# Loading a routed layer's expert matrices, router and bias row during the attention before it

## The chip, the cores and the metric

The kernel runs on one core of a Trainium2 chip. The metric is the device time of one execution in microseconds (us). Times of the profile are counted from the first instruction of the profiled execution. TensorE is called PE here, VectorE DVE, ScalarE ACT, GpSimd POOL and SyncE SP. SP, ACT and POOL can each issue DMA transfers on a queue of their own (SPq is q1, ACTq is q10).

## The reference

A sequence of 32 batches of 112 tokens with 256 features passes through four layers. Each adds a gated cross attention over a context of 375 rows, and a gated feed-forward part. Only the last layer's two parts and their order matter here:

```python
def _L3_xattn_ref(q, k, v, mask, gamma, beta):          # q: layernorm(x), k = v = context
    logits = jnp.einsum('bsd,btd->bst', q, k) / jnp.sqrt(d_k)
    logits = jnp.where(mask == 0, NEG, logits)
    attn = jax.nn.softmax(logits, axis=-1)
    x = jnp.einsum('bst,btd->bsd', attn, v)
    ...                                                  # layernorm over features
    return xhat * gamma + beta

def _L3_ffn_ref(tokens, router_w, router_b, expert_weights):   # 8 experts of 256 x 256
    logits = jnp.einsum('bsh,eh->bse', tokens, router_w) + router_b
    probs = jax.nn.softmax(logits, axis=-1)
    top_p, top_i = jax.lax.top_k(probs, TOP_K)           # TOP_K = 2
    w = top_p / (jnp.sum(top_p, axis=-1, keepdims=True) + EPS)
    ...
    y_all = jnp.einsum('nh,ehd->ned', x, expert_weights)
    y_k = jnp.take_along_axis(y_all, idx[:, :, None], axis=1)
    out = jnp.einsum('nk,nkh->nh', wf, y_k)
    ...
x = x + jnp.tanh(g_xattn[3]) * _L3_xattn_ref(_layernorm(x), ctx_1024, ctx_1024, mask, ...)
x = x + jnp.tanh(g_ffn[3]) * _L3_ffn_ref(_layernorm(x), router_w, router_b, expert_weights)
```

## The kernel before

x stays in SBUF for the whole program, as `x_sb` with 112 tokens on the partitions and 32 batches of 256 features. Each part of each layer is a function with one or more blocks. In a block every engine has its own hand-written list of instructions, tied to the others by semaphores; at the end of a block all engines wait for each other, and only then does the next block begin. Storage and semaphores of a function are given back at its end (`cleanup_on_exit`). All numbers are float32.

`masked_attention` (line 528) is the fourth attention. PE's list runs over the batches j: transpose the normalised x of batch j + 1 (line 763), transpose the probabilities of batch j - 2 (782), scores of batch j (773), attention product of batch j - 2 (793). DVE masks the scores (651, 655), takes the statistics of the result (663, 665, 667), adds the residual of batch j - 4 (675), normalises batch j + 4 (642) and takes the statistics of batch j + 10 (633, 635). ACT turns the mask into a number (706, 710), does the exponentials (723), and copies the two transposes out of PSUM (717, 731). POOL raises to the power of -1/2 (597 and 599 for groups of four batches, 612, 615, 617 for each result) and adds beta (606).

Its transfers: SP loads for each pair of batches one mask (line 578, 328 KB, three buffers) and for each batch the transposed context `ctx_t` (line 583, 375 KB, four buffers). The load of ctx_t of batch j waits until the scores of batch j - 4 are done. ACT loads the context `ctx_sb` itself (line 736, 384 KB, eight buffers), after the attention product that frees the buffer. That goes on for the last eight batches too, and SP waits at the end of its list (line 590) until all have landed. At its start ACT loads the rows gamma and beta (738, 739), and waits for POOL's `masked` and for the first mask.

`routed_layer` (line 2756) has two blocks. The first, small one prepares: SP issues eight expert matrices into `we` (2776, 256 KB each), ACT loads the router as 8 rows of 256 (2780) and the bias row, repeated on 112 partitions (2781); POOL writes the numbers 0 to 7 (2786), DVE turns them into floats (2791); PE transposes the router (2799), DVE copies it to `rw_t` (2793). The second block is the layer: DVE takes the statistics of 16 batches (2857, 2860), POOL the power (2840, 2842), DVE normalises (2871), PE transposes (2994) and multiplies by the router (3003), ACT copies (2983), DVE finds the two best experts and their weights, then PE multiplies each batch by all eight experts (3015) while DVE adds the weighted results (2935). The other 16 batches are normalised and routed in between.

Of the kernel before, what the change touches and what calls it, by code (L numbers as in the profile page):

```python
# [4 lines left out]
F32 = mybir.dt.float32  # L5
U32 = mybir.dt.uint32
I32 = mybir.dt.int32
# [47 lines left out]
def row(v):  # L55

    return v.rearrange("(a n) -> a n", a=1)
# [470 lines left out]
def masked_attention(k):  # L528
# [8 lines left out]
    with nc.cleanup_on_exit():  # L537
# [34 lines left out]
        with nc.Block() as block:  # L572
            @block.sync
            def _(sp):
# [10 lines left out]
                for j in range(B):  # L585
                    if j % 2 == 0:
                        load_masks(j // 2)
                    load_ctx_t(j)
                for j in range(NB):
                    sp.wait_ge(ctx_loaded[j], 16 * (B // NB))  # L590

            @block.gpsimd
            def _(pool):
# [25 lines left out]
                pool.memset(masked[:, :], MASKED).then_inc(s["masked_ready"], 1)  # L619
                norm_scale(0)  # L620
# [81 lines left out]
            def _(act):  # L702
# [36 lines left out]
                act.dma_start(beta[:, :], row(k.inputs["L3_xattn_beta"]).partition_broadcast(S)).then_inc(s["rows_loaded"], 16)  # L739
                act.wait_ge(s["masked_ready"], 1)  # L740
# [2011 lines left out]
E3 = 8  # L2752
WEIGHT_EPS = 1e-10


def routed_layer(k):
# [3 lines left out]
    with nc.cleanup_on_exit():  # L2760
        we = sb(nc, "we", [P, DC, E3, D], F32)
        rw_t = sb(nc, "rw_t", [P, DC, E3], F32)
        rb = sb(nc, "rb", [S, E3], F32)
        iota = sb(nc, "iota", [S, E3], F32)
        experts_loaded = sem(nc, "experts_loaded")
        with nc.cleanup_on_exit():
            router_loaded = sem(nc, "router_loaded")
            transposed = sem(nc, "transposed")
            iota_ready = sem(nc, "iota_ready")
            rw = sb(nc, "rw", [E3, D], F32)  # L2770
            iota_i = sb(nc, "iota_i", [S, E3], I32)
            with nc.Block() as block:
                @block.sync
                def _(sp):
                    for e in range(E3):
                        sp.dma_start(we[:, :, e, :], k.inputs["L3_ffn_expert_weights"][e]).then_inc(experts_loaded, 16)

                @block.scalar
                def _(act):
                    act.dma_start(rw[:, :], k.inputs["L3_ffn_router_w"]).then_inc(router_loaded, 16)  # L2780
                    act.dma_start(rb[:, :], row(k.inputs["L3_ffn_router_b"]).partition_broadcast(S)).then_inc(router_loaded, 16)
                    act.wait_ge(router_loaded, 32)

                @block.gpsimd
                def _(pool):
                    pool.iota(iota_i[:, :], pattern=[[1, E3]], base=0, channel_multiplier=0).then_inc(iota_ready, 1)

                @block.vector
                def _(dve):
                    dve.wait_ge(iota_ready, 1)  # L2790
                    dve.tensor_copy(iota[:, :], iota_i[:, :])
                    dve.wait_ge(transposed, 1)
                    dve.tensor_copy(rw_t[:, :, :], k.ps[:, 0, 0:DC * E3].rearrange("p (c e) -> p c e", c=DC))

                @block.tensor
                def _(pe):
                    pe.wait_ge(router_loaded, 32)
                    for c in range(DC):
                        mm = pe.transpose(k.ps[:, 0, c * E3:(c + 1) * E3], rw[:, c * P:(c + 1) * P], k.ident[0:E3, 0:E3])
                    mm.then_inc(transposed, 1)  # L2800

# [26 lines left out]
        with nc.Block() as block:  # L2828
# [16 lines left out]
            def _(dve):  # L2845
# [27 lines left out]
                def shift_logits(g):  # L2873
                    cut = slice(g * BODY, (g + 1) * BODY)
                    dve.wait_ge(s["logits_done"], BODY * (g + 1))
# [112 lines left out]
            def _(pe):  # L2988
# [8 lines left out]
                def route(j):  # L2997
                    pe.wait_ge(s["xt_copied"], j + 1)
                    if j >= BODY:
                        pe.wait_ge(s["exps_ready"], j // BODY)  # L3000
# [133 lines left out]
```

## Time and profile before

| | |
|---|---|
| median of 3 runs | 3386.21 us (3382.05 to 3387.3) |
| the profiled execution's own time | 3380.2 us |
| its span, first to last instruction | 3378.5 us |
| busy, share of the span | PE 91%, DVE 60%, ACT 43%, POOL 19% |
| mean granted TensorE clock | 0.947 of full speed |
| the fourth attention's block | 2972.37 to about 3095 us |
| the routed layer's first block | 3096.08 to about 3101.3 us |
| the routed layer's second block | 3102.86 to 3378.5 us |

The profile is one execution; the time of its own stands beside the span so that a difference in the profile can be carried over to the runs. The rows of the next section come from the trace of that execution. A row of the timeline is: start in us, duration in us, engine, line, operation, written tile <- read tiles, shapes, how many instructions were merged, and in brackets the idle time of the engine before it and what ended it. "PEld" is PE's weight load; SPq and ACTq are transfers being issued (the duration is that of issuing, not of moving the data).

### The profile page before, as it was taken

The page shows a single profiled execution, that of the slowest core. Times are in us where ns is not written, and L with a number is a line of the kernel's source. Part 1 is how long each engine was busy: PE and PEld are TensorE (multiplying, and loading weights), DVE is VectorE, ACT ScalarE, POOL GpSimd, SP SyncE. Part 2 cuts the span into 40 slices and gives each one's busy share as a digit, 9 for nine tenths or more (in the row PEclk, how much of TensorE's full clock was granted, in tenths as well). Part 3 has the DMA queues.
Part 4 walks back from the last instruction along what each step waited for, and adds up shares of the span by engine and source line. Part 5 has one row for each costly group of instructions (what it writes and reads, how often), then busy time and mean ns, then how long its engine had stood idle before and what let it go on. Part 6 is the DMA issues. An engine that isn't in the chain of part 4 may idle for free. (4 is left out here: it accounts for less than half of the span.)

```text
span 3378.5 us, 61456 instructions
## 1 busy us (share of the span) xinstructions
PE 3073.2 (91%) x23644; PEld 2339.1 (69%) x23644; DVE 2032.5 (60%) x4425; ACT 1444.9 (43%) x2808; POOL 644.0 (19%) x903
## 2 busy tenths in 40 slices
PE   8986699967789999999999999499999999797999
PEld 6864355634588999999999999366667666465443
DVE  3444211128537788778778777266666666587554
ACT  3421111103325555555555555166666666354000
POOL 3443100028300013012001300411111111144000
PEclk9986799988899999999999999699999999798899
DMA  7661111127710000000000000100000000075000
GB/s 237 190 249 48 51 50 50 50 78 226 256 40 1 2 1 2 1 1 2 2 1 2 2 1 2 39 20 20 20 20 20 20 20 11 4 210 178 12 15 19
DMA packets 75489, 183.40 MB, mean 54 GB/s; under 512 B 12215, under 2 KB 18960, under 8 KB 74866
## 3 DMA queue, kind: packets, MB, share of 16 engines
q1 hardware_dynamic: 56452, 135.91, 12.6%
q10 hardware_dynamic: 12606, 29.06, 2.8%
q0 software_dynamic: 6144, 14.50, 1.5%
q8 instruction: 194, 3.18, 0.4%
q14 instruction: 93, 0.76, 0.1%
HBM read 151.83 MB, written 27.79 MB: 53 GB/s over the span
## 5 line engine op out<-in xcount | busy, mean ns | idle before, releaser
L2313 DVE CUSTOM_DVE_ANT_0 probs<-ps,add 112x375 f32<-112x375 f32 x512 | 250.1, 545 | 58.4 <-PE ps L2441 54.6
L2369 ACT ACTIVATE probs<-probs,neg_top 112x375 f32<-112x375 f32 x512 | 281.7, 599 | 4.6 <-DVE neg_top L2313 3.2
L1864 DVE TENSOR_REDUCE top<-ps 112x16 f32<-112x1792 f32 x96 | 194.4, 2025 | 60.0 <-PE ps L2080 58.4
L3015 PE MATMUL ps<-we,xn_t 128*112 128x512 f32 x512 | 226.9, 605 | 0.5 <-DVE x_sb L2935 0.5
L1217 DVE TENSOR_TENSOR hidden<-gated,ps 128x512 f32<-128x512 f32 x64 | 44.0, 688 | 301.8 <-PE ps L1260 301.8
L2466 PE MATMUL ps<-ident,probs 112*125 112x112 f32 x1536 | 222.5, 281 | 2.8 <-DVE probs_t L2320 2.8
L2320 DVE COPY probs_t<-ps 125x336 f32<-125x336 f32 x256 | 128.9, 504 | 151.4 <-PE ps L2466 151.4
L2466 PEld LDWEIGHTS ps<-ident,probs 112*125 112x125 f32 x1536 | 189.7, 188 | 30.8 <-issue 22.6
L1880 DVE TENSOR_TENSOR probs<-probs,inv_sum 112x1792 f32<-112x1792 f32 x96 | 194.4, 2025 | 3.3
L1868 DVE TENSOR_TENSOR probs<-ps,top 112x1792 f32<-112x1792 f32 x96 | 194.3, 2024 | 3.3
L1876 DVE TENSOR_REDUCE row_sum<-probs 112x16 f32<-112x1792 f32 x96 | 193.9, 2020 | 3.2 <-ACT probs L1966 3.2
L2048 PE MATMUL ps<-ident,probs 112*112 112x112 f32 x1536 | 180.5, 260 | 8.0 <-ACT probs_t L1961 7.3
L2063 PE MATMUL ps<-nodes,wq 128*128 128x224 f32 x768 | 182.9, 361 | 4.4
L3015 PEld LDWEIGHTS ps<-we,xn_t 128*112 128x112 f32 x512 | 92.5, 182 | 131.8 <-issue 115.5
L1961 ACT ACTIVATE probs_t<-ps 112x896 f32<-112x896 f32 x192 | 176.0, 917 | 15.6 <-PE ps L2048 4.3
L2039 PE MATMUL ps<-wv,nodes 128*112 128x256 f32 x768 | 181.4, 379 | 0.0
L2048 PEld LDWEIGHTS ps<-ident,probs 112*112 112x112 f32 x1536 | 162.9, 134 | 25.8 <-issue 8.0
L2065 PE MATMUL ps<-att_t,wo 128*128 128x224 f32 x768 | 177.4, 354 | 0.0
L2019 PE MATMUL ps<-nodes,wkh 128*128 128x224 f32 x768 | 172.5, 368 | 0.0
L2935 DVE SCALAR_TENSOR_TENSOR x_sb<-ps,weight,x_sb 112x256 f32<-112x256 f32 x256 | 110.6, 478 | 99.0 <-PE ps L3015 98.7
L1857 DVE COPY v<-ps 112x512 f32<-112x512 f32 x96 | 66.4, 692 | 171.3 <-PE ps L2039 171.3
L2375 ACT ACTIVATE probs_t<-ps 125x336 f32<-125x336 f32 x256 | 115.2, 450 | 125.8 <-PE ps L2466 124.2
(402 smaller groups left out, 6388.0 us busy)
## 6 DMA issues: line engine op xcount, KB each, us to landing
ctx_t<-in_ctx_T_dram SPq DMA_DIRECT2D x128, 375.0 KB, 3.4
ctx_sb<-in_ctx_dram ACTq DMA_DIRECT2D x72, 384.0 KB, 4.9
ctx_sb<-in_ctx_dram SPq DMA_DIRECT2D x32, 384.0 KB
queue<-zeros SPq DMA_DIRECT2D x32, 256.0 KB, 4.2
rows<-queue SPq DMA_DIRECT2D x16, 512.0 KB, 4.2
outputs<-out SPq DMA_DIRECT2D x16, 512.0 KB, 2.6
mask_in<-in_mask_BxSxS_fk_dram SPq DMA_DIRECT2D x16, 328.1 KB, 4.3
mask_in<-in_mask_BxSxS_ik_dram SPq DMA_DIRECT2D x16, 328.1 KB
```

The costliest lines, as they stand in the source:

```text
L1864: dve.tensor_reduce(top[:, :, :], scores, AX.X, ALU.max).then_inc(s["top_done"], 1)
L1868: dve.tensor_tensor(probs[:, m % 2, :, :, :], scores, top[:, :, :].unsqueeze(3).broadcast_to([S, 4, PAIR * HQ, S]), ALU.subtract).then_inc ...
L1876: dve.tensor_reduce(row_sum[:, :, :], p, AX.X, ALU.add).then_inc(s["sum_done"], 1)
L1880: dve.tensor_tensor(p, p, inv_sum[:, :, :].unsqueeze(3).broadcast_to([S, 4, PAIR * HQ, S]), ALU.mult).then_inc(s["probs_normed"], 1)
L2039: mm = pe.matmul(k.ps[0:S, ODD, b * D:(b + 1) * D], node_v[:, i, b * S:(b + 1) * S], w.wv[:, c, i, :], start=i == 0, stop=i == DC - 1)
L2048: mm = pe.transpose(k.ps[0:S, PT + h // 4, h % 4 * S:(h % 4 + 1) * S], probs[:, m % 2, h % 4, b * HQ + h // 4, :], k.ident[0:S, 0:S])
L2063: pe.matmul(k.ps[:, ODD, a * PS:(a + 1) * PS], w.wq[:, c, i, cut], node_q[:, i, :], start=i == 0, stop=False)
L2065: mm = pe.matmul(k.ps[:, ODD, a * PS:(a + 1) * PS], w.wo[:, c, i, cut], att_t[:, i, :], start=False, stop=i == DC - 1)
L2313: dve.tensor_tensor_reduce(out=probs[:, u, h, :], in0=k.ps[0:S, SCORE + h, 0:L], in1=add[:, j % 2, :], scale=1.0, scalar=BIG, op0=ALU.add, ...
L2369: act.activation(probs[:, u, h, :], probs[:, u, h, :], ACT.Exp, bias=neg_top[:, u, h:h + 1], scale=-1.0).then_inc(s["probs_done"], 1)
L2466: mm = pe.transpose(k.ps[0:KR, PT + h % 2, r * S:(r + 1) * S], probs[:, n % 3, h, r * KR:(r + 1) * KR], k.ident[0:S, 0:S])
L3015: mm = pe.matmul(k.ps[0:S, Y + at % YB, :], xn_t[:, j + u, c, :], we[:, c, e:e + TWO, :].rearrange("p e d -> p (e d)"), start=c == 0, stop ...
```

## The change

The storage of the expert matrices, the router, the bias row and the numbering is allocated before the fourth attention instead of after it. SP issues one expert matrix after each ctx_t of batches 17, 19, ... 31. ACT issues router and bias row at the start of the attention, behind gamma and beta. POOL writes the numbering there and turns it into floats itself. The router is laid out transposed by the host, as 128 partitions of 2 x 8 numbers, so that PE's two transposes and DVE's copy fall away. The routed layer's first block is gone; its second block waits for the loads where it first uses them.

```diff
--- before.py
+++ after.py
@@ -525,7 +525,26 @@
                         attend(j - 2)
 
 
-def masked_attention(k):
+E3 = 8
+WEIGHT_EPS = 1e-10
+
+
+def routed_storage(k, r):
+
+
+    nc = k.nc
+    r.we = sb(nc, "we", [P, DC, E3, D], F32)
+    r.rw_t = sb(nc, "rw_t", [P, DC, E3], F32)
+    r.rb = sb(nc, "rb", [S, E3], F32)
+    r.iota = sb(nc, "iota", [S, E3], F32)
+    r.iota_i = sb(nc, "iota_i", [S, E3], I32)
+    r.experts_loaded = sem(nc, "experts_loaded")
+    r.router_loaded = sem(nc, "router_loaded")
+    r.iota_ready = sem(nc, "iota_ready")
+    r.iota_copied = sem(nc, "iota_copied")
+
+
+def masked_attention(k, r):
 
 
     nc = k.nc
@@ -586,6 +605,9 @@
                     if j % 2 == 0:
                         load_masks(j // 2)
                     load_ctx_t(j)
+                    if j >= B - 2 * E3 and j % 2:
+                        e = (j - B + 2 * E3) // 2
+                        sp.dma_start(r.we[:, :, e, :], k.inputs["L3_ffn_expert_weights"][e]).then_inc(r.experts_loaded, 16)
                 for j in range(NB):
                     sp.wait_ge(ctx_loaded[j], 16 * (B // NB))
 
@@ -617,6 +639,9 @@
                     pool.tensor_tensor(gain[:, cut], sum_sq[:, cut], k.neg_half[0:S, 0:1], ALU.pow).then_inc(s["gain_done"], 1)
 
                 pool.memset(masked[:, :], MASKED).then_inc(s["masked_ready"], 1)
+                pool.iota(r.iota_i[:, :], pattern=[[1, E3]], base=0, channel_multiplier=0).then_inc(r.iota_ready, 1)
+                pool.wait_ge(r.iota_ready, 1)
+                pool.tensor_copy(r.iota[:, :], r.iota_i[:, :]).then_inc(r.iota_copied, 1)
                 norm_scale(0)
                 norm_scale(1)
                 for j in range(B + LAG):
@@ -737,6 +762,8 @@
 
                 act.dma_start(gamma[:, :], row(k.inputs["L3_xattn_gamma"]).partition_broadcast(S)).then_inc(s["rows_loaded"], 16)
                 act.dma_start(beta[:, :], row(k.inputs["L3_xattn_beta"]).partition_broadcast(S)).then_inc(s["rows_loaded"], 16)
+                act.dma_start(r.rw_t[:, :, :], k.inputs["L3_ffn_router_w"]).then_inc(r.router_loaded, 16)
+                act.dma_start(r.rb[:, :], row(k.inputs["L3_ffn_router_b"]).partition_broadcast(S)).then_inc(r.router_loaded, 16)
                 act.wait_ge(s["masked_ready"], 1)
                 add_mask(0)
                 copy_xn(0)
@@ -2749,56 +2776,11 @@
                 pipeline(PAIRS, [(transpose, 0), (add_bias, 1), (multiply, 1)])
 
 
-E3 = 8
-WEIGHT_EPS = 1e-10
-
-
-def routed_layer(k):
+def routed_layer(k, r):
 
 
     nc = k.nc
     with nc.cleanup_on_exit():
-        we = sb(nc, "we", [P, DC, E3, D], F32)
-        rw_t = sb(nc, "rw_t", [P, DC, E3], F32)
-        rb = sb(nc, "rb", [S, E3], F32)
-        iota = sb(nc, "iota", [S, E3], F32)
-        experts_loaded = sem(nc, "experts_loaded")
-        with nc.cleanup_on_exit():
-            router_loaded = sem(nc, "router_loaded")
-            transposed = sem(nc, "transposed")
-            iota_ready = sem(nc, "iota_ready")
-            rw = sb(nc, "rw", [E3, D], F32)
-            iota_i = sb(nc, "iota_i", [S, E3], I32)
-            with nc.Block() as block:
-                @block.sync
-                def _(sp):
-                    for e in range(E3):
-                        sp.dma_start(we[:, :, e, :], k.inputs["L3_ffn_expert_weights"][e]).then_inc(experts_loaded, 16)
-
-                @block.scalar
-                def _(act):
-                    act.dma_start(rw[:, :], k.inputs["L3_ffn_router_w"]).then_inc(router_loaded, 16)
-                    act.dma_start(rb[:, :], row(k.inputs["L3_ffn_router_b"]).partition_broadcast(S)).then_inc(router_loaded, 16)
-                    act.wait_ge(router_loaded, 32)
-
-                @block.gpsimd
-                def _(pool):
-                    pool.iota(iota_i[:, :], pattern=[[1, E3]], base=0, channel_multiplier=0).then_inc(iota_ready, 1)
-
-                @block.vector
-                def _(dve):
-                    dve.wait_ge(iota_ready, 1)
-                    dve.tensor_copy(iota[:, :], iota_i[:, :])
-                    dve.wait_ge(transposed, 1)
-                    dve.tensor_copy(rw_t[:, :, :], k.ps[:, 0, 0:DC * E3].rearrange("p (c e) -> p c e", c=DC))
-
-                @block.tensor
-                def _(pe):
-                    pe.wait_ge(router_loaded, 32)
-                    for c in range(DC):
-                        mm = pe.transpose(k.ps[:, 0, c * E3:(c + 1) * E3], rw[:, c * P:(c + 1) * P], k.ident[0:E3, 0:E3])
-                    mm.then_inc(transposed, 1)
-
         stats = sb(nc, "stats", [S, B, 6], F32)
         mean_var = sb(nc, "mean_var", [S, B, 2], F32)
         var_eps = sb(nc, "var_eps", [S, B], F32)
@@ -2873,8 +2855,10 @@
                 def shift_logits(g):
                     cut = slice(g * BODY, (g + 1) * BODY)
                     dve.wait_ge(s["logits_done"], BODY * (g + 1))
+                    if g == 0:
+                        dve.wait_ge(r.router_loaded, 32)
                     link(dve.tensor_tensor(logits[:, cut, :], k.ps[0:S, LOGITS, 0:BODY * E3].rearrange("p (g e) -> p g e", g=BODY),
-                                           rb[:, :].unsqueeze(1).broadcast_to([S, BODY, E3]), ALU.add))
+                                           r.rb[:, :].unsqueeze(1).broadcast_to([S, BODY, E3]), ALU.add))
                     link(dve.tensor_reduce(top[:, cut], logits[:, cut, :], AX.X, ALU.max))
                     link(dve.tensor_tensor(logits[:, cut, :], logits[:, cut, :], each(top[:, cut]), ALU.subtract))
                     dve.sem_inc(s["exps_ready"], 1)
@@ -2899,7 +2883,9 @@
 
                 def pick(g):
                     cut = slice(g * BODY, (g + 1) * BODY)
-                    every = iota[:, :].unsqueeze(1).broadcast_to([S, BODY, E3])
+                    if g == 0:
+                        dve.wait_ge(r.iota_copied, 1)
+                    every = r.iota[:, :].unsqueeze(1).broadcast_to([S, BODY, E3])
                     dve.tensor_tensor(route1[:, cut, :], every, each(best_f[:, cut, 0]), ALU.is_equal)
                     link(dve.tensor_tensor(weight[:, cut, :], every, each(best_f[:, cut, 1]), ALU.is_equal))
                     link(dve.tensor_tensor(weight[:, cut, :], weight[:, cut, :], route1[:, cut, :], ALU.add))
@@ -2996,11 +2982,13 @@
 
                 def route(j):
                     pe.wait_ge(s["xt_copied"], j + 1)
+                    if j == 0:
+                        pe.wait_ge(r.router_loaded, 32)
                     if j >= BODY:
                         pe.wait_ge(s["exps_ready"], j // BODY)
                     at = j % BODY * E3
                     for c in range(DC):
-                        mm = pe.matmul(k.ps[0:S, LOGITS, at:at + E3], xn_t[:, j, c, :], rw_t[:, c, :], start=c == 0, stop=c == DC - 1)
+                        mm = pe.matmul(k.ps[0:S, LOGITS, at:at + E3], xn_t[:, j, c, :], r.rw_t[:, c, :], start=c == 0, stop=c == DC - 1)
                     mm.then_inc(s["logits_done"], 1)
 
                 def experts(j):
@@ -3012,7 +3000,7 @@
                                 pair, w = divmod(before, E3)
                                 pe.wait_ge(s["added"], pair * E3 * 2 + (w // 2 * TWO + TWO - 1) * 2 + w % 2 + 1)
                             for c in range(DC):
-                                mm = pe.matmul(k.ps[0:S, Y + at % YB, :], xn_t[:, j + u, c, :], we[:, c, e:e + TWO, :].rearrange("p e d -> p (e d)"),
+                                mm = pe.matmul(k.ps[0:S, Y + at % YB, :], xn_t[:, j + u, c, :], r.we[:, c, e:e + TWO, :].rearrange("p e d -> p (e d)"),
                                                start=c == 0, stop=c == DC - 1)
                             mm.then_inc(s["experts_done"], 1)
 
@@ -3021,7 +3009,7 @@
                         transpose(j)
                     if j:
                         route(j - 1)
-                pe.wait_ge(experts_loaded, 16 * E3)
+                pe.wait_ge(r.experts_loaded, 16 * E3)
                 for j in range(0, BODY, 2):
                     experts(j)
                     if 4 <= j < 8:
@@ -3068,8 +3056,10 @@
         searched_network(k)
         many_headed_attention(k)
         ternary_layer(k)
-        masked_attention(k)
-        routed_layer(k)
+        r = Fields()
+        routed_storage(k, r)
+        masked_attention(k, r)
+        routed_layer(k, r)
         finish(k)
 
 
@@ -3094,6 +3084,8 @@
 
     if name in _BY_CHUNK:
         a = a.reshape(a.shape[:-2] + (-1, P, a.shape[-1])).swapaxes(-3, -2)
+    elif name == "L3_ffn_router_w":
+        a = a.T.reshape(-1, P, a.shape[0]).swapaxes(0, 1)
     elif name in _COLUMNS:
         a = a.reshape(a.shape[:-1] + (-1, P)).swapaxes(-2, -1)
     elif name in _MASKS:
```

`Fields` is an empty class that holds attributes. In the host's arrangement `_arranged`, arrays in `_BY_CHUNK` (the expert matrices among them) already have 128 rows on the partitions.

## Rows read from the trace of the kernel before

**Rows 1.** The page's chain by engine; then the chain in order of time, from 3040 us

```profile
PE 7%; DVE 1%; POOL 0%; issue 0%; ACT 0%; DVEq 0%
...
3102.81 0.04 issue
3102.86 0.75 DVE stats L2857 x2
```

**Rows 2.** Timeline, end of the attention and the routed layer's first block

```profile
3089.91 2.43 ACTq L736 DMA_DIRECT2D ctx_sb<-in_ctx_dram  x2
3090.46 1.52 PE L793 MATMUL ps<-ctx_sb,probs_t 125*112 125x256 f32 x6 [0.59 <-issue]
3094.01 0.48 DVE L675 SCALAR_TENSOR_TENSOR x_sb<-o_scaled,gain,x_sb 112x256 f32<-112x256 f32 x1 [0.44 <-POOL gain L617]
3096.08 5.24 SPq L2776 DMA_DIRECT2D we<-_ffn_expert_weights_dram  x8
3096.09 0.14 POOL L2786 IOTA iota_i<- 112x8 int32 x1 [2.11 <-POOLq L537]
3096.41 0.34 ACTq L2781 DMA_DIRECT2D rb<-in_L_ffn_router_b_dram  x1
3100.26 0.38 PE L2799 MATMUL ps<-ident,rw 8*128 8x8 f32 x2 [8.29 <-DMA rb<-in_L_ffn_router_b_dram]
3100.68 0.17 DVE L2793 COPY rw_t<-ps 128x16 f32<-128x16 f32 x1 [4.24 <-PE ps L2799]
```

**Rows 3.** SP's waits at line 590: duration ns min/median/max, first and last start us

```profile
L590 SPq EVENT_SEMAPHORE  x4: 17/28/28, 3089.6 to 3094.9; - x4
```

**Rows 4.** Timeline, start of the attention's block

```profile
2972.77 0.45 ACTq L739 DMA_DIRECT2D beta<-in_L_xattn_beta_dram  x1
...
2974.72 0.24 POOL L597 TENSOR_SCALAR var_eps<-mean_var 112x4 f32<-112x4 f32 x1 [2.25 <-DVE mean_var L635]
...
2976.90 0.52 ACT L706 ACTIVATE size<-mask_in 112x375 f32<-112x375 int32 x1 [11.31 <-DMA mask_in<-in_mask_BxSxS_ik_dram]
...
2979.03 2.81 PE L773 MATMUL ps<-ctx_t,xn_t 128*112 128x375 f32 x4 [1.44 <-DMA ctx_t<-in_ctx_T_dram]
```

**Rows 5.** ACT's queue, 3096 to 3110 us, then 2971 to 2980: packets, MB, share

```profile
q10 hardware_dynamic: 144, 0.01, 0.9%
...
q10 hardware_dynamic: 256, 0.23, 13.1%
```

**Rows 6.** Windows: us, busy us (x) of PE PEld DVE ACT POOL, PEclk, DMA share, GB/s

```profile
3020.00:3070.00 50.00, 49.55 (x218) 34.32 (x217) 47.13 (x140) 34.43 (x90) 33.28 (x66) 1.00 0.92 277
3060.00:3070.00 10.00, 10.00 (x48) 7.46 (x47) 8.72 (x25) 7.29 (x19) 7.12 (x15) 1.00 0.97 297
3070.00:3080.00 10.00, 10.00 (x48) 7.46 (x47) 8.34 (x25) 6.88 (x18) 5.80 (x13) 1.00 0.72 227
3101.00:3104.00 3.00, 0.00 (x0) 0.00 (x0) 1.15 (x6) 0.00 (x0) 0.00 (x0) 0.50 1.09 363
```

**Rows 7.** Timeline: mask and ctx_t issues of the steady state, and their users

```profile
3021.12 4.00 SPq L583 DMA_DIRECT2D ctx_t<-in_ctx_T_dram  x2
3066.57 0.43 SPq L578 DMA_DIRECT2D mask_in<-in_mask_BxSxS_ik_dram  x1
3069.47 3.59 SPq L583 DMA_DIRECT2D ctx_t<-in_ctx_T_dram  x2
3078.37 0.51 ACT L706 ACTIVATE size<-mask_in 112x375 f32<-112x375 int32 x1
3081.09 1.43 PE L773 MATMUL ps<-ctx_t,xn_t 128*112 128x375 f32 x4
```

**Rows 8.** DMA issues, 3020 to 3092 us: count, KB, median us to landing

```profile
ctx_sb<-in_ctx_dram ACTq DMA_DIRECT2D x23, 384.0 KB, 3.8
```

**Rows 9.** Windows as in rows 6: the clock at the seam and in the routed layer

```profile
3094.00:3095.00 1.00, 0.00 (x0) 0.00 (x0) 0.48 (x1) 0.00 (x0) 0.00 (x0) 0.65 0.28 108
3179.00:3180.00 1.00, 1.00 (x11) 1.00 (x11) 0.64 (x2) 0.65 (x2) 0.00 (x0) 0.82 0.00 0
3179.64:3186.46 6.82, 6.82 (x26) 4.79 (x26) 0.83 (x2) 1.43 (x4) 0.00 (x0) 0.50 0.00 0
```

## The prediction

> **What bounds the kernel now.** I read the page first. Its chain that ended last holds only about 8% of the span [rows 1], and the time order of that chain says why: its first piece is at 3102.81 us, right ahead of the first statistics instruction of the routed layer. What lies before is separated from it by the end of a block, where every engine waits for every other and no single releaser is recorded. So the program is a row of blocks, and the change touches two of them and the seam between them. All before 2970 us stays as it is, and so does the body of the routed layer: it starts with vector statistics at 3102.86 [rows 1] and runs until 3378.5. Time can change in three places: the start of the fourth attention, its steady state, and the seam.
>
> Then the timeline of the seam [rows 2]. PE's last product of the attention ends at 3091.98; its last vector work, the residual of batch 31, runs 3094.01 to 3094.49. SP leaves its last wait, for the last context transfer, at 3094.9 [rows 3], so this transfer and not an engine ends the block, and 1.2 us later (3096.08) SP, ACT and POOL begin the small inner block. There ACT issues the router and the bias row, PE has to wait 8.3 us until the bias row has landed, transposes at 3100.26, VectorE copies at 3100.68. SP meanwhile spends 5.24 us on issuing eight expert transfers, until 3101.32. After that 1.49 us pass to 3102.81. Two chains are therefore almost equally long: load, transpose, copy (until 3100.85) and SP's issuing (until 3101.32). The change removes both; taking away only one would have bought next to nothing.
>
> Last the attention block, for what the moved work meets there: the start [rows 4], and the busy windows of the steady state [rows 6]. Between 3020 and 3070 PE is busy 49.55 of 50 us and VectorE 47.13, so they set the pace, but the DMA engines are busy 0.92 of the time, 0.97 in the last ten of these. That is where moved transfers could hurt.
>
> **The change part by part.**
>
> *The seam.* The inner block goes wholly: two PE transposes, two copies on VectorE, one iota, ten DMA issues and one block end. If the routed layer's block starts where the inner block started, the gain is 3102.81 - 3096.08 = 6.73 us. What could differ is the price of the seam: 1.2 us from SP's release to the first instruction at this one, 1.49 us from SP's last issue at the next. With the larger one the gain is 6.4. I take 6.7, since the block that ends before the routed layer is now the attention's own, whose 1.2 us stand in the trace. The last context transfer still gates it: it is on ACT's queue, issued by 3092.34 (3089.91 + 2.43, [rows 2]), when all experts have long been loaded.
>
> *ACT's two moved issues* go behind gamma and beta, whose issues end at 2973.22 (2972.77 + 0.45, [rows 4]). Two issues of about 0.34 us [rows 2] end at 2973.9. Behind them on ACT is the first mask operation, at 2976.90 and waiting for its transfer: 3.0 us of cover, cost nothing. Uncovered they would cost 0.7.
>
> *Their packets.* The router is now 128 pieces of 64 bytes, the row 112 of 32 bytes: 240 packets, 15 on each of 16 engines. They compete with the first ctx_t, for which PE stands idle at 2979.03 [rows 4], so this is on the path. Price of a packet: in the inner block ACT's queue had 144 such small ones for 0.9% of 16 engines over 14 us, 14 ns each; at the attention's start 256 of mostly 1 KB took 13.1% of 9 us, 74 ns each [rows 5]. That gives 0.2 to 1.1 us. I take 0.2, because the first row is the row of this very bias transfer.
>
> *POOL's iota and copy* (0.14 us [rows 2] and, as the nearest row, 0.24 for a 112x4 operation [rows 4]) with a wait between them end by about 2973.1. Behind them is the epsilon addition of the first norm scale, at 2974.72 and waiting for VectorE. Cover 1.6 us, cost nothing; uncovered 0.4, and even then xn would only be later at a PE which waits until 2979.03 anyway.
>
> *SP's eight expert issues*, 0.655 us each (5.24 / 8, [rows 2]), come behind ctx_t of batches 17, 19, ... 31, from about 3025 (the pair of rows that starts with batch 16 is issued from 3021.12 for 4.00 us, [rows 7]) to 3073. Each stands ahead of a mask load and of SP's wait for the next scores. The last mask is issued at 3066.57 and used by ACT at 3078.37, the ctx_t of batch 30 issued at 3069.47 and used by PE at 3081.09 [rows 7]: 11.8 and 11.6 us, of which a transfer of this size takes 3.8 to land [rows 8]. Some 7.8 us are spare; 0.66 is nothing.
>
> *Their bytes* are the doubtful term. Seven of them, 1.84 MB, fall in 3025 to 3070: 41 GB/s on top of 277, so 318 GB/s. At 277 GB/s for a share of 0.92 [rows 6] full use is 301 GB/s; 17 GB/s too few over 45 us leaves 0.76 MB, and transfers would be 2.5 us late by 3070. At 3070 to 3080 the load falls to 0.72 and the backlog drains. 2.5 is less than 7.8, so PE sees nothing: cost 0. The other end is that the full engine time of 2.10 MB, 7.0 us at 301 GB/s, comes through to PE. I take the low end, as experts by themselves ran at 363 GB/s [rows 6], so 301 is a cautious limit. The Trainium skill ("Trainium Kernel Development and Optimization", Key Constraints) speaks against this part: transfers issued from SP, ACT and POOL all run on the same 16 engines and interleave, so another queue gives no bandwidth. The share of 0.92 with two queues bears it out. "DMA: Bandwidth & Descriptors" (Specifications) puts the memory's limit for one core at about 358 GB/s; by that figure there would be no backlog at all and the sum the same, by the row's 301 there is one of 2.5 us, hidden.
>
> *New waits* (one on PE, two on VectorE) find semaphores that are set long before; SP's like instructions show 17 to 28 ns [rows 3]. Under 0.1 us in all, nothing taken.
>
> **Sum.** -6.7 + 0.2 = -6.5 us. The profiled execution took 3380.2 us, which makes 3373.7. The median of the runs, 3386.21, is 6.0 above that execution and becomes 3379.7, or 0.19% less. Three runs of one kernel lie 0.16% apart (3382.05 to 3387.3), so about 0.2%, 6.8 us, is what a measurement of this kernel can tell from no change. The forecast sits just under that line.
>
> **Rivals.**
>
> *Contention leaks.* Between 2 and 7 us of the expert transfers' engine time reach PE, as waits of the scores for ctx_t. For it: the shares of 0.92 and 0.97. Against it: 7.8 us of spare lead, and transfers that land in 3.8 us under the present load [rows 8]. With the middle, 4.5 us, the time is 3384.2.
>
> *Clock steps.* In the routed layer the granted clock falls from 1.00 to 0.50 (from 2.4 to 1.2 GHz) twice for 6.8 us, the first time from 3179.64 to 3186.46 [rows 9], after a stretch of small transposes and routing products. PE is saturated there, so each costs half its length, 3.4 us. If the earlier start makes one more, the time is 3383.1; if it saves one, 3376.3. For it: what stands before a fall is a thin stretch of PE work, and such a stretch needs to be only slightly thinner or denser. Against it: the body of the layer is the same instruction by instruction, and after the seam PE is cold in both (its idle stretch goes from 21 to about 14.5 us, and before it fell inside 3094 to 3095 [rows 9], within 3 us of its last product). The Trainium skill ("TensorE: Matmul & The Clock Gate", the part on the clock gate) says that the activity watch is free-running, so that one kernel's slow matmuls vary from run to run; no row of a single execution can show that.
>
> *The end on the other side.* ctx_t comes late often enough that PE stops at each expert, and the clock falls too. It decides when a ctx_t needs more than the 11.6 us of lead, three times what it takes now. Then all 7.0 us come through and, with two falls of 3.4, 13.8: 3386.2 - 6.5 + 13.8 = 3393.5.
>
> *The seam is not shortened*: the 1.49 us and the wait for code or for the barrier are owed to the start of the routed layer itself and come on top of the attention's own seam. Then 1.5 us of the 6.7 stay, and the time is 3381.2. For it: the unexplained difference of 0.3 between the two seams. Against it: the seam at 3096.08 is one full block end and costs 1.2.
>
> **How the numbers follow.** Forecast 0.60 (own range 3377 to 3383, from the 1.1 us bound of the packets, the 0.3 of the seam and half the spread of the runs); contention leaks 0.12; one clock step more 0.08, one less 0.08; seam not shortened 0.07; slower side 0.05. Leaving out the last, and of the others the outer ends (a full leak of 7.0 us, a saved step on top of a fast median), gives 3375 to 3386; that leaves about 0.15 outside. Faster by over 0.2%, that is under 3379.4: a little under half of the forecast (0.27), all of the saved clock step (0.08) and 0.05 from the other cases by the scatter of the medians: 0.40. Slower by over 0.2%, over 3393.0: 0.03, most of the case on the other side. Within: 0.57.
>
> **What would show it.** Right: no matmul or copy between the attention's last residual and the first statistics, and that gap 1.6 us instead of 8.4; expert transfers from about 3025 on; PE without waits for ctx_t; DMA share near 1 from 3025 to 3070; the attention's residual of batch 31 ending within 0.5 us of 3094.5. Wrong: PE waits on ctx_t or ACT on mask_in after 3025, a seam of over 2 us, ctx_t first used later than 2979.5, or a third cold stretch in the routed layer.

## The result, and the profile after

The changed kernel takes 3379.1 us (median of 17 runs, 3374.8 to 3381.64) against 3383.64 for the kernel before (17 runs beside it, 3381.18 to 3387.3): ratio 0.9982, 95% interval 0.9975 to 0.9989, or 6.1 us less, between 3.7 and 8.5. The two medians alone differ by 4.5 us. Its profiled execution has a span of 3373.0 us, 5.5 less than before.

The timeline at the seam, changed kernel, answering to [rows 2]:

```profile
3090.78 2.43 ACTq L761 DMA_DIRECT2D ctx_sb<-in_ctx_dram  x2
...
3094.88 0.48 DVE L700 SCALAR_TENSOR_TENSOR x_sb<-o_scaled,gain,x_sb 112x256 f32<-112x256 f32 x1 [0.44 <-POOL gain L639]
3097.39 0.75 DVE L2839 BATCH_NORM_STATS2 stats<-x_sb 112x6 f32<-112x256 f32 x2 [2.03 <-PEq L556]
```

SP's last wait there, answering to [rows 3]:

```profile
L612 SPq EVENT_SEMAPHORE  x4: 17/28/28, 3090.6 to 3096.2; - x4
```

The start of the attention, where ACT issues four rows, POOL numbers and copies, and PE takes up the first scores, answering to [rows 4]:

```profile
2973.54 0.43 DVE L658 BATCH_NORM_STATS2 stats<-x_sb 112x6 f32<-112x256 f32 x1 [0.87 <-PEq L2605]
2973.55 0.14 POOL L642 IOTA iota_i<- 112x8 int32 x1
2973.76 0.19 POOL L644 CAST iota<-iota_i 112x8 f32<-112x8 int32 x1
...
2974.86 0.45 ACTq L766 DMA_DIRECT2D rb<-in_L_ffn_router_b_dram  x1
...
2975.86 0.24 POOL L619 TENSOR_SCALAR var_eps<-mean_var 112x4 f32<-112x4 f32 x1 [1.91 <-DVE mean_var L660]
...
2979.90 2.81 PE L800 MATMUL ps<-ctx_t,xn_t 128*112 128x375 f32 x4 [1.16 <-ACT xn_t L742]
```

Two windows of the steady attention, answering to [rows 6], and one of SP's new issues:

```profile
3020.00:3070.00 50.00, 49.46 (x219) 34.44 (x218) 47.44 (x141) 33.85 (x89) 33.24 (x66) 1.00 0.98 303
3060.00:3070.00 10.00, 10.00 (x47) 7.41 (x46) 9.04 (x26) 7.47 (x20) 6.93 (x15) 1.00 1.00 320
```

```profile
3026.03 0.66 SPq L610 DMA_DIRECT2D we<-_ffn_expert_weights_dram  x1
```

Four pieces make up the 5.5 us of the spans. I measure each from an instruction that both kernels have. Up to the attention's first statistics nothing is changed, and the changed kernel is 1.13 us late (2973.54 against 2972.41). The attention, first statistics to last residual, takes 121.82 against 122.08, 0.26 less. The seam takes 2.03 (3095.36 to 3097.39) against 8.37 (3094.49 to 3102.86), 6.34 less. The routed layer from its first statistics on takes 275.61 against 275.64. So 1.13 - 0.26 - 6.34 - 0.03 = -5.5. The 1.13 is scatter: in nine executions of the groups in which the kernel before takes some 3385 us, of kernels that are the same up to there, the attention's first statistics began between 2972.4 and 2979.7 us. That is more than the change is worth, and the reason why the experiments below are read by stages and not by spans.

### The profile page after: what moved, and what is told of

Read it like the earlier page. It is cut to its first block and busy times, and to the rows that moved or that the text cites. A ratio compares the mean times of both kernels' runs of the same rounds, so it can differ in the third digit from the quotient of the medians.

```text
span 3373.0 us, 61429 instructions
## 1 busy us (share of the span) xinstructions
PE 3067.9 (91%) x23642; PEld 2335.7 (69%) x23642; DVE 2032.2 (60%) x4423; ACT 1445.8 (43%) x2808; POOL 645.3 (19%) x904
```

## The experiments

Kernels were run in groups, each beside runs of the kernel before on the same chip. The kernel before takes some 3385 us in some of the groups and 3357 to 3360 in others, so that spans are compared only within a group; stages agree across them. This table gives for each execution: attention from first statistics to last residual; seam from there to the routed layer's first statistics; SP's last wait after the end of the last context issue; and the routed layer from its first statistics.

| | attention | seam | last wait | routed layer |
|---|---|---|---|---|
| before | 122.08 | 8.37 | 2.6 | 275.6 |
| before again | 121.97 | 8.48 | 2.7 | 275.7 |
| the change | 121.82 | 2.03 | 3.0 | 275.6 |
| the change again | 121.85 | 2.13 | 3.1 | 275.5 |
| experts moved alone | 121.83 | 6.71 | 3.2 | 277.3 |
| router moved alone | 121.98 | 8.84 | 3.1 | 275.6 |
| experts in the routed block | 121.98 | 2.26 | 3.2 | 275.5 |
| extra block end | 122.08 | 3.32 | 3.0 | 277.2 |
| no unused context | 121.86 | 1.02 | - | 275.9 |
| experts twice | 128.62 | 2.17 | 3.2 | 275.6 |
| experts four times | 139.05 | 2.24 | 3.2 | 275.5 |
| experts twice, spread | 121.66 | 2.18 | 3.2 | 275.6 |
| small loads eight times | 126.42 | 1.70 | 2.7 | 278.4 |

The last kernel below, statistics early, has no statistics at the head of its routed layer and is described by itself. Where the routed layer took over 277 us, a stretch at half clock lasted longer (*the clock steps*, below).

**Experts moved alone.** The router's path stays in a block of its own, as in the kernel before.

```diff
-                pool.iota(r.iota_i[:, :], ...)
-                act.dma_start(r.rw_t[:, :, :], ...)
-                act.dma_start(r.rb[:, :], ...)
+            with nc.Block() as block:     # before the routed layer's block
+                    act.dma_start(rw[:, :], k.inputs["L3_ffn_router_w"]).then_inc(router_loaded, 16)
+                    act.dma_start(r.rb[:, :], ...).then_inc(router_loaded, 16)
...
```

> The expert matrices are loaded during the attention as in the change, but router, bias row and numbering keep the small block of their own, with PE's transposes and VectorE's copies. Theory (the gain is the seam, where two chains ran side by side, SP's issuing of 5.24 us and the bias row's load, transpose and copy of about 4.8 us): taking away SP's alone leaves the other, so from the attention's last residual to the first statistics there are still about 6.5 to 8 us instead of 8.4, and the kernel is 0.5 to 1.8 us faster than before. Rival (the expert loads were the costly part, since the bias row's transfer of 3.5 KB only took so long because it shared the queues with them): the gap falls to under 6 us and at least half of the 6.3 us is had.

Ratio to before 1.0002 (0.9992 to 1.0011). The timeline of this kernel's small block:

```profile
3098.23 0.33 ACTq L2788 DMA_DIRECT2D rb<-in_L_ffn_router_b_dram  x1
3100.61 0.38 PE L2806 MATMUL ps<-ident,rw 8*128 8x8 f32 x2 [7.49 <-DMA rb<-in_L_ffn_router_b_dram]
3101.03 0.17 DVE L2800 COPY rw_t<-ps 128x16 f32<-128x16 f32 x1 [2.77 <-PE ps L2806]
3102.35 0.75 DVE L2864 BATCH_NORM_STATS2 stats<-x_sb 112x6 f32<-112x256 f32 x2 [1.15 <-PEq L2779]
```

The seam keeps 6.71 of 8.37 us. The bias row was used 2.4 us after its issue here against 3.9 with the experts in flight [rows 2], so the rival is right that the transfers hindered each other, but only by 1.5 us; the seam stays over 6. Experts alone earn a quarter of the seam's gain. The expected 0.5 to 1.8 us of the whole time did not show: by the interval, anything from 2.7 us less to 3.7 more is possible, and the profiled execution had one of the longer stretches at half clock.

**Router moved alone.** The small block holds only SP's eight issues.

```diff
-                    if j >= B - 2 * E3 and j % 2:      # in the attention
...
+                    for e in range(E3):                # in a block of its own
+                        sp.dma_start(r.we[:, :, e, :], ...).then_inc(r.experts_loaded, 16)
```

> The other half alone: router, bias row and numbering come from the attention as in the change, and a small block between the two layers holds nothing but SP's issuing of the eight expert transfers. Theory (either chain alone holds the seam): the small block lasts 5.24 us for the issuing and 1.5 us for its end, so from the last residual to the first statistics there are about 8.4 us again, as in the kernel before, give or take 0.5 for the landing of the last context transfer; the run is within 0.1% of before. Rival (the router's path was the longer chain): the gap is under 7.5 us.

Ratio 0.9995 (0.9986 to 1.0005), seam 8.84. The timeline shows SP's issues and what follows the block's end:

```profile
3103.78 5.23 SPq L2787 DMA_DIRECT2D we<-_ffn_expert_weights_dram  x8
```

```profile
3110.47 0.75 DVE L2844 BATCH_NORM_STATS2 stats<-x_sb 112x6 f32<-112x256 f32 x2 [8.84 <-PEq L2781]
```

From the end of SP's issuing, 3109.01, to these statistics at 3110.47 it is 1.46 us, against 1.54 in the kernel before (3101.32 to 3102.86). SP's issuing alone holds the whole seam: each chain was enough for most of it, and only moving both gives it up.

**Experts in the routed block.** The change, but with the eight issues at the head of SP's list in the routed layer's block.

```diff
-                    if j >= B - 2 * E3 and j % 2:      # in the attention
...
             def _(sp):                                 # routed layer
+                for e in range(E3):
+                    sp.dma_start(r.we[:, :, e, :], ...).then_inc(r.experts_loaded, 16)
                 for j in range(0, B, 2):
```

> Router, bias row and numbering are prepared in the attention, no small block, but SP issues the eight expert transfers at the start of the routed layer's own block, ahead of its waits for stores. Theory: nothing waits for the end of the issuing or for the transfers (PE needs them some 27 us later, they take about 10), so the gap stays at about 2.0 us and the time is that of the change within 0.3 us in the trace; DMA share of the steady attention back at 0.92. If the transfers in the attention had cost something hidden there, this one would be faster in the attention's block by that.

Ratio 0.9978 (0.9968 to 0.9988), seam 2.26, DMA share back at 0.91 in the attention, whose length does not move. The span was expected within 0.3 us of the change's and is 2.2 longer, of which 1.9 lie ahead of the attention, where the kernels are the same. So what counted was that no block ends behind the issues, not that the attention carries them.

**Extra block end.** The change with a further block that does nothing.

```diff
+            with nc.Block() as block:
+                    sp.sem_inc(seam, 1)
+                    sp.wait_ge(seam, 1)
```

> The changed kernel with one more block between attention and routed layer in which only SP sets a semaphore and waits for it. It prices one block with its end and the release of its semaphore. Theory (a block end costs 1.2 us from the last engine's arrival): the gap from the last residual to the first statistics goes from 2.03 to 3.1 to 3.4 us. Rival (the gap of 2.03 is owed to the start of the routed layer, such as its code): under 0.5 us more.

Seam 3.32, 1.2 to 1.3 us more than 2.03 and 2.13, from one execution: that is one block end, as far as one execution can show it, and the rival (under 0.5) falls.

**No unused context.** The change without the last eight context loads.

```diff
-                    sp.wait_ge(ctx_loaded[j], 16 * (B // NB))
+                    sp.wait_ge(ctx_loaded[j], 16 * (B // NB - 1))
...
-                    if 0 <= j - LAG < B:
+                    if 0 <= j - LAG < B - NB:
                         load_ctx(j - LAG + NB)
```

> The changed kernel without the attention's last eight context loads, which nothing reads. Theory (the gap of 2.03 us begins with a wait of SP for the last of these transfers, which lands 0.8 us after the last residual): the gap falls to 1.2 to 1.4 us, 0.6 to 0.8 us less, too small for the timed runs. Rival (the end of the block itself takes 2.0 us from the last vector instruction): the gap stays at 2.0.

Ratio to before 0.998 (0.997 to 0.9989), no different from the change. In the timeline the seam is halved, to 1.02, where 1.2 to 1.4 had been expected:

```profile
3098.20 0.48 DVE L700 SCALAR_TENSOR_TENSOR x_sb<-o_scaled,gain,x_sb 112x256 f32<-112x256 f32 x1 [0.44 <-POOL gain L639]
3099.70 0.75 DVE L2839 BATCH_NORM_STATS2 stats<-x_sb 112x6 f32<-112x256 f32 x2 [1.01 <-PEq L556]
```

**Experts twice, experts four times.** Further copies go to spare storage.

```diff
+                        for n in range(1):             # or range(3)
+                            sp.dma_start(r.spare[:, n, :, e, :], ...).then_inc(r.spare_loaded, 16)
```

> The changed kernel with each expert matrix loaded twice in the attention, the second time into spare storage: 16 transfers, 82 GB/s on top of 277 between 3025 and 3070 us. If 301 GB/s is the limit, as the share of 0.92 at 277 GB/s suggested, transfers come 8.7 us late by 3070, more than the 7.8 spare, and PE waits about 1 us or more for ctx_t. If the limit is the 363 GB/s of the experts by themselves, no wait and the attention's block is as long as in the change (121.4 us from its start to the last residual).

> The changed kernel with each expert matrix loaded four times: 32 transfers, 164 GB/s on top of 277, 441 in all. Any limit under 441 must show now. With 363 GB/s transfers are 9.7 us late by 3070, and PE waits some 2 to 5 us; with 301 they are 21 us late and PE waits 13 us or more. No wait at all would mean that the transfers never compete for what the attention waits for.

The attention is 6.8 and 17.2 us longer than in the change. In the waits of the first of the two, ACT stands idle for masks (us in all, times, longest):

```profile
ACT size L735 <- DMA mask_in<-in_mask_BxSxS_ik_dram: 10.2, 5, 2.5
...
PE ps L804 <- issue: 4.8, 4, 1.4
```

Its windows in the stretch of the added transfers:

```profile
3015.00:3025.00 10.00, 10.00 (x45) 6.83 (x44) 9.59 (x30) 6.43 (x18) 6.88 (x15) 1.00 1.05 301
3025.00:3035.00 10.00, 8.80 (x41) 6.40 (x40) 9.21 (x28) 6.24 (x16) 6.34 (x12) 1.00 1.05 301
```

The rate stands at 301 GB/s with the share at 1.05, just the limit that the share of 0.92 had suggested, and the added 2.10 MB at 301 GB/s are 7.0 us, of which 6.8 came through. My 1 us was far too low: the spare 7.8 us were not there. The times to landing show why, of masks, ctx_t and ctx_sb in this order (us, min/median/max). In the kernel before, second trace, whose times are 21 us earlier, 3020 to 3070:

```profile
DMA to landing us min/median/max: 4.7/5.0/5.6
...
DMA to landing us min/median/max: 3.5/4.6/5.3
...
DMA to landing us min/median/max: 2.9/3.7/5.9
```

With the experts twice, the same window:

```profile
DMA to landing us min/median/max: 15.1/15.7/16.2
...
DMA to landing us min/median/max: 12.2/13.9/14.9
...
DMA to landing us min/median/max: 3.6/8.0/8.6
```

The window of the kernel before takes in the attention's emptier end; in its steady stretch, 2999 to 3049, the medians are 5.6, 4.8 and 4.5. SP's queue, in which the experts lie ahead of the masks, carried most of the backlog: 15.7 us for a mask, more than its 11.8 of lead [rows 7], while ACT's queue took 8.0. With four times as many the rate reached 329 GB/s, and 441 were asked; 6.3 MB more cost 17.2 us, as at 366 GB/s, part of them in the attention's end, where the engines have room (0.72 in [rows 6]). Here the clock fell as well, behind a stretch in which PE stood idle for a third of the time:

```profile
3025.00:3035.00 10.00, 6.77 (x30) 4.95 (x30) 7.82 (x24) 4.95 (x14) 5.64 (x11) 1.00 1.06 329
3035.00:3045.00 10.00, 9.44 (x34) 6.51 (x34) 5.66 (x16) 5.62 (x17) 4.22 (x10) 0.83 1.07 329
```

That is the prediction's case on the other side, at four times the bytes; how much of the 17.2 us is clock is not measured.

**Experts twice, spread.** 16 transfers, one behind each odd batch.

```diff
-                    if j >= B - 2 * E3 and j % 2:
+                    if j % 2:
...
```

> As many bytes as in the run with each expert matrix loaded twice (16 transfers), but one behind ctx_t of every odd batch from 1 to 31 instead of two behind each from 17 on. Theory (what PE waited for there was the rate in SP's queue, over what the engines can move, from batch 17 on): 41 GB/s more over the whole attention fits, so the attention lasts 121.8 us from its first statistics to its last residual, give or take 0.5. Rival (each transfer beyond the first eight costs its engine time of about 0.87 us wherever it lies): 128.6 us as in that run.

The attention takes 121.66 us: the second set of loads cost nothing. The rate was 317 GB/s between 2995 and 3020 and 307 between 3020 and 3070, with PE busy 49.47 of 50 us. What costs is the rate above what the engines move, not the bytes.

**Small loads eight times.** Router and bias row are loaded eight times at the attention's start.

```diff
+                for n in range(8):
+                    act.dma_start(r.rw_t8[:, n, :, :], ...)
+                    act.dma_start(r.rb8[:, n, :], ...)
```

> The changed kernel with the router and the bias row each loaded eight times at the attention's start (spare copies): 1920 small packets instead of 240, 120 on each engine. It prices these packets where PE waits for the first ctx_t. At 14 ns each the first scores come 1.5 us later than in the change, at 74 ns each 7.8 us later; 6.4 us from the block's start in the change. No shift at all would mean that the engines serve the other queue's packets without loss, and that 0.2 us was too much for the change too. The attention's first masks wait on ACT, which issues 16 transfers instead of 2: 14 more at 0.45 us are 6.3 us, so ACT may become the first bound, at 7.5 us after the block's start.

First scores come 10.98 us after the first statistics, against 6.36. But it is ACT, later than the 7.5 us expected, since its 16 issues took 0.54 us each on average: they last until 2955.49, its first mask operation follows at 2955.60, where the page's releaser is "issue", and PE waits for its xn_t. As a price of packets on PE's path the run is inconclusive. The queue gives one (packets, MB, share of 16 engines; this kernel, 2945 to 2960 us):

```profile
q10 hardware_dynamic: 2053, 0.31, 14.2%
```

34 us of engine time in all; less 224 packets of gamma and beta at the 74 ns of [rows 5], 17.5 us are left for 1829 small ones, 10 ns each, near the 14 I had taken.

**The change again, the kernel before again.**

> The changed kernel once more, for what one and the same kernel shows from execution to execution. Theory of the scatter: the routed layer's block took 275.6 us in five of these traces and 277.2 to 278.4 in three, because a stretch at half clock lasted 10.2 us instead of 6.9; this varies by execution and not by kernel, so the block takes between 275.5 and 278.5 here, the attention 121.8 from first statistics to last residual, and the gap after it 2.0 to 2.3.

> The kernel before once more. In its first trace SP's wait ended 2.6 us after the last context transfer had been issued (3092.34 to 3094.9 us); in seven traces of changed kernels it was 3.0 to 3.2. If 2.6 is a property of the kernel before, the gap from the last residual to the routed layer's first statistics is 8.4 us here again, and the change saves 6.3. If it was the luck of one execution, the landing takes 3.0 to 3.2 here too, the gap is 8.8, and the change saves about 6.7 as predicted.

Both repeat their first traces: seams of 2.13 and 8.48 us. So in either pair the change saves 6.34 or 6.35, not 6.7. But that the short landing, 2.6 to 2.7 us, is a property of the kernel before does not follow: the run with the small loads is a changed kernel, its last transfer landed after 2.7 too, and its seam is 1.70, 6.7 less than before. In the nine other traces of changed kernels it was 3.0 to 3.2.

**Statistics early.** The version without unused context loads, which also takes the statistics of the routed layer's first 16 batches in the attention, one batch per step from 18 on, with the powers in groups of four on POOL.

```diff
+                    if 0 <= j - EARLY < BODY:          # DVE, attention; EARLY = 18
+                        next_statistics(j - EARLY)
...
+                    if j > EARLY and (j - EARLY) % GROUP == 0 and (j - EARLY) // GROUP <= BODY // GROUP:
+                        next_scale((j - EARLY) // GROUP - 1)      # POOL
...
-                for j in range(BODY):                  # DVE, routed layer
-                    statistics(j)
-                last_mean(BODY - 1)
```

> A version that may beat both: the changed kernel without the eight unused context loads, and with the routed layer's statistics of batches 0 to 15 (and their powers on POOL, in groups of four) taken during the attention, one batch per step from step 18 on, when that batch's residual is done. Theory (the 6.4 us of statistics and 3.4 us of POOL stand alone at the head of the routed layer): the first transpose comes about 1.7 us after the attention's last residual instead of 12.4, that is 10.6 us less; VectorE pays 16 times 0.5 us in the attention, where it has some 0.45 us of slack per step from step 22 on, so 2 to 4 us come back as a longer attention. Net 6.5 to 8.5 us faster than the change, near 3371 us. Rival (the attention is so tight on VectorE that all 8 us come back, and POOL's powers delay its results): within 2 us of the change.

Ratio to before 0.9959 (0.9945 to 0.9973), some 13.8 us less: faster than the kernel before, and by the two ratios than the change. The end of its attention:

```profile
3069.04 0.48 DVE L726 SCALAR_TENSOR_TENSOR x_sb<-o_scaled,gain,x_sb 112x256 f32<-112x256 f32 x1 [0.44 <-POOL gain L653]
3069.32 1.12 POOL L635 TENSOR_TENSOR r_rstd<-r_var_eps,neg_half 112x4 f32<-112x4 f32 x1
3071.84 0.73 DVE L2882 TENSOR_SCALAR xn<-x_sb,r_mean_var,r_rstd 112x256 f32<-112x256 f32 x2 [2.31 <-PEq L563]
```

From the last residual to the first normalisation it is 2.32 us against 11.92 in the change; the attention is 123.73 against 121.82. Net 9.6 - 1.9 = 7.7 us, inside what was expected, though both parts came out one lower than expected (10.6, and 2 to 4). Some 1.0 of it is the unused context's, as in the run above.

## Why the prediction was right

*The whole.* 6.5 us were forecast, 6.1 measured (3.7 to 8.5), 3379.7 against 3379.1 us. Both are under the 0.2% line, where the most likely side was put. That the two times lie so close is partly luck: the forecast started from the median of three runs, 3386.21, and 17 runs put it at 3383.64, from which the same 6.5 us give 3377.1, 2.0 below the measured median. By stages the two traces say 6.6 (0.26 in the attention, 6.34 in the seam, 0.03 behind it).

*The seam, 6.73 forecast, 6.34 measured.* The mechanism held. That the two chains were nearly equal, and one of them worth next to nothing alone, is shown: 1.7 us for the one, none for the other. The mis-sized part is how long the context's last transfer takes: 3.0 us instead of 2.6, so SP's wait ends later. In the one changed kernel where it took 2.7 the seam is 1.70, near the 1.64 forecast. From that wait's end to the first instruction it is 1.2 us in both, as taken, and an added block end costs as much. The rival of a seam that is not shortened is out.

*The packets, 0.2 forecast, nothing measured.* First scores come 6.36 and 6.43 us after the first statistics, against 6.62 and 6.53 before. In the first trace of the change they wait for xn_t, in the second still for ctx_t, as before:

```profile
2981.31 2.81 PE L800 MATMUL ps<-ctx_t,xn_t 128*112 128x375 f32 x4 [1.23 <-DMA ctx_t<-in_ctx_T_dram]
```

The engine time was about right (10 ns a packet), but no delay of the first scores shows.

*ACT's and POOL's moved work, nothing forecast.* Held: ACT's issues took 0.45 us each instead of 0.34 and end at 2975.31, POOL's copy at 2973.95 (0.19 us), ahead of the next work of their engines at 2978.15 and 2975.86. With eight times the loads ACT's cover is gone and 4.6 us appear.

*The bytes, nothing forecast.* The result held: the attention takes 121.82 us with the experts in it and 121.98 without (experts in the routed block), and after 3025 no wait of PE for ctx_t or of ACT for a mask is left among the waits. The share went to 0.98 and 1.00 as said. The backlog was there too: 305 GB/s instead of the 318 asked between 3025 and 3070 leave some 0.6 MB (0.76 forecast), and between 3070 and 3080 the engines moved 303 GB/s, against 227 before (26 of the difference are the eighth expert). But the reasoning had a flaw. I took the time to landing of ctx_sb, 3.8 us, for masks and ctx_t, which are in the other queue, the one the experts were put into. At twice the bytes that queue's masks took 15.7 us and not 3.8 plus a little, and my expectation of 1 us became 6.8. The change passed with less to spare than the 7.8 us claimed. Its own trace lists no landing times, but the run with the small loads carries the same experts in its attention, and its masks between 3000 and 3048 show

```profile
DMA to landing us min/median/max: 6.4/6.6/8.3
```

against 5.6 at the median in the kernel before. Of the 11.8 us of lead, 5.2 were spare at the median and 3.5 at the worst. The rule of the Trainium skill ("Trainium Kernel Development and Optimization", Key Constraints) that SP's and ACT's transfers share the engines fits: with the experts twice ACT's own transfers went from 3.7 to 8.0 us (from 4.5 in the steady stretch). The row's 301 GB/s was a little low as a limit: this mix reached 320 in the change (share 1.00) and 329 with four times the experts. The 358 GB/s of the Trainium skill ("DMA: Bandwidth & Descriptors", Specifications) it reached in no stretch of 10 us shown here.

*The clock steps.* In the pair of traces both stretches at half clock lasted the same, so they explain nothing of the result. But the rival exists: in "experts moved alone", in "extra block end" and in the run with the small loads the first stretch was 10.2 us, in the last of them the second as well, and the layer was 1.6 to 2.8 us longer. It came in 3 of the 14 traces and in neither of two of the change. What brings it is open.

*The signs.* Two signs of being wrong came up by their numbers: the seam is 2.03 and 2.13 us, just over the 2 named (1.6 was forecast), for the landing above; and ctx_t is first used at 2979.90, later than 2979.5. The second, and the last residual's end at 3095.36 instead of within 0.5 of 3094.5, come from the 1.13 us by which the whole attention began late: a time counted from the start of the program was no usable sign, with a scatter of 7 us. The other signs of being right held: no work between the last residual and the statistics, expert transfers from 3026.03 on, two cold stretches and not three.

## What to carry to other kernels

Ask of every block how long its longest chain is, and how long the second: here two independent ones of nearly one length held a seam of 8.4 us, and either move alone bought at most 1.7. Issues count as a chain too: a block ends only when SP has issued its last transfer, though nobody waits for the data. When loads are moved under other work, weigh them by rate over the stretch and look at the time to landing in the queue they are put into; spread thin a second set of them was free, bunched it cost its full 7 us.

## What was not expected

The last context transfer landed 2.6 and 2.7 us after its issue in the two traces of the kernel before and 2.7 in one of a changed kernel, but 3.0 to 3.2 in nine of changed kernels, also where nothing about that transfer was changed (router moved alone: 3.1). The three short ones share one thing: the load two before it was issued by 6.9 us ahead of the last residual's end, in the nine others by 6.5 to 6.7. Whether that is the cause is not shown. And eight transfers that nothing reads held the seam open by 1.0 us.
